# Two FP4 feed-forward stages: quantisation spread over three engines and the gated values quantised two steps later

## The chip, the cores and the metric

The program runs on one core of a Trainium2 chip. The metric is the device time of one execution in microseconds (us). The engines are named as the profile names them: PE is TensorE, PEld its weight loads, DVE VectorE, ACT ScalarE, POOL GpSimd, SP SyncE.

## What is computed

Six stages run one after the other on an activation of 16 x 256 tokens of width 128, each with a layer norm before it and a residual add behind it: an FP4 feed-forward, a low-rank attention, the same FP4 feed-forward again, a mixture of experts, a second attention, the mixture of experts again. The change touches the first and the third stage:

```python
def fp4_quant_dequant(x):                    # blocks of 16 along the last dim
    xb = x.reshape(shape[:-1] + (shape[-1] // BLOCK, BLOCK))
    scale = jnp.maximum(jnp.max(jnp.abs(xb), axis=-1, keepdims=True) / 6.0, 1e-12)
    xn = xb / scale
    idx = jnp.searchsorted(_MID, jnp.abs(xn))
    return (_GRID[idx] * jnp.sign(xn) * scale).reshape(shape)
def fp4_linear(x, w):
    return jnp.einsum('bsk,nk->bsn', fp4_quant_dequant(x), fp4_quant_dequant(w))
gate = fp4_linear(x, w_gate)                 # 128 -> 352
y = fp4_linear(x, w_up)                      # 128 -> 352
h = jax.nn.silu(gate) * y
return fp4_linear(h, w_down)                 # 352 -> 128; x + 0.5 * this
```

## The kernel before

The 4096 tokens are 32 tiles of 128 rows that stay in SBUF (`k.X`). Class `Ffn` handles two tiles at a time, so a run of the stage has N = 16 pairs, and it is called twice (`run` 0 and 1). Every engine has its own program, and semaphores tie them together; the order on each engine is the order in which the code is written. Between two stages all engines meet.

Step z works on the normalised values x of pair z (256 columns) and on the gated values h of pair z - 2 (704 columns) side by side in one buffer of 960 columns, `k.xh`:

- VectorE multiplies silu and the up projection into h (L248), then `quantise` runs over all 960 columns: block maximum (L101), scale (L104), reciprocal (L105), nudge (L106), multiply (L107), absolute value as an integer mask (L114), `max` with the magic number (L115), rounding add (L116). Then it adds the down projection of pair z - 3 to X (L265) and takes its statistics (L184).
- GpSimd subtracts the magic number (L140) and multiplies by the scale (L142), both over 960 columns, into `k.xhq`.
- TensorE transposes x (L293) and h (L299), multiplies by gate and up (L307, into PSUM) and by down (L316).
- ScalarE normalises the next x (L328), copies the transposes to SBUF (L343, L348, L349) and applies silu (L354).

There is one buffer each for the input of quantisation, for the quotient `xn`, for the magnitude `mg` and for the scale. The scale of step z may be written only after GpSimd has ended step z - 1 (`s_scaled`, the wait ahead of L104). A run takes 18 steps.

Of the kernel before, what the change touches and what calls it, by code (L numbers as in the profile page):

```python
# [130 lines left out]
QD = 6  # L131
# [61 lines left out]
class Ffn:  # L193
# [4 lines left out]

    N = NT // 2
    XC, HC_, ALL = (0, 2 * D), (2 * D, 2 * D + 2 * I0), (0, 2 * D + 2 * I0)  # L200

    def __init__(self, k, run):

        self.k, self.run = k, run
        self.x0 = run * self.N
        self.q0 = run * (self.N + 2)
        self.s_xn = k.sem("ffn_xn")
        self.s_xn_read = k.sem("ffn_xn_read")
        self.s_rounded = k.sem("ffn_rounded")
        self.s_minus = k.sem("ffn_minus")  # L210
        self.s_scaled = k.sem("ffn_scaled")
# [10 lines left out]
    def rounds(self, eng, fn, ch=None, per=0):  # L222

        n = self.N
        fn(0, True, False, False)
        fn(1, True, False, False)
        fn(2, True, True, False)
        with eng.Fori(3, n - 1) as z:
            if ch:
                ch.enter(z - 3, per)  # L230
            fn(z, True, True, True)
            if ch:
                ch.leave(n - 4)
        fn(n - 1, True, True, True)
        fn(n, False, True, True)
        fn(n + 1, False, True, True)

    def cols(self, x, h):
        return self.ALL if x and h else self.XC if x else self.HC_

    def vector(self, eng, ch):
        k, v = self.k, self.k.nc.vector
        x0, q0 = self.x0, self.q0

        def fn(z, x, h, back):
            if h:
                eng.wait_ge(self.s_silu, x0 + z - 1)
                v.tensor_tensor(k.xh[:, 2 * D:].rearrange("p (a b) -> p a b", a=2), k.sg[:, :, :],  # L248
                                k.PS[:, 2:4, 0:I0], ALU.mult).then_inc(self.s_h, 1)
                eng.wait_ge(self.s_h, x0 + z - 1)  # L250
# [20 lines left out]
    def gpsimd(self, eng, ch):  # L271
        k = self.k
        x0, q0 = self.x0, self.q0

        def fn(z, x, h, back):
            eng.wait_ge(self.s_rounded, q0 + z + 1)
            if x and (not isinstance(z, int) or z or self.run):
                eng.wait_ge(self.s_xqT_ps, x0 + z)
            if back or (h and self.run):
                eng.wait_ge(self.s_hqT_ps, x0 + z - 2)  # L280
            dequantise(k.nc, k.xhq, k.qt, self.cols(x, h), (self.s_minus, q0 + z + 1), self.s_scaled)

        self.rounds(eng, fn)

    def tensor(self, eng):
        k, t = self.k, self.k.nc.tensor
        x0, q0 = self.x0, self.q0

        def fn(z, x, h, back):
            eng.wait_ge(self.s_scaled, q0 + z + 1)  # L290
            if x:
                for j in range(2):
                    last = t.transpose(k.PS[:, 4, j * P:(j + 1) * P], k.xhq[:, j * D:(j + 1) * D], k.ident[:, :])  # L293
                last.then_inc(self.s_xqT_ps, 1)
            if h:
                for j in range(2):
                    for c, (o, w) in enumerate(HC):
                        o += 2 * D + j * I0
                        last = t.transpose(k.PS[0:w, 5 + j, c * P:(c + 1) * P], k.xhq[:, o:o + w], k.ident[:, :])  # L299
                last.then_inc(self.s_hqT_ps, 1)  # L300
            if x:
                eng.wait_ge(self.s_xqT, x0 + z + 1)
                if not isinstance(z, int) or z or self.run:
                    eng.wait_ge(self.s_h, x0 + z)
                for j in range(2):
                    for w, bank in ((0, 0), (1, 2)):
                        last = t.matmul(k.PS[:, bank + j, 0:I0], k.xqT[:, j * P:(j + 1) * P], k.wguT[:, w, :],  # L307
                                        start=True, stop=True)
# [12 lines left out]

    def scalar(self, eng):
        k, s = self.k, self.k.nc.scalar
        x0, n = self.x0, self.N

        def normalised(i):
            for j in range(2):
                ins = s.activation(k.xh[:, j * D:(j + 1) * D], k.X[:, ds(2 * i + j, 1), :].squeeze(1), ACT.Identity,  # L328
# [4 lines left out]
        normalised(0)  # L333

        def fn(z, x, h, back):
            if x:
                if not (isinstance(z, int) and z == n - 1):
                    eng.wait_ge(self.s_xn_read, x0 + z + 1)
                    normalised(z + 1)
                eng.wait_ge(self.s_xqT_ps, x0 + z + 1)  # L340
                if not isinstance(z, int) or z or self.run:
                    eng.wait_ge(self.s_gu_ps, x0 + z)
                s.activation(k.xqT[:, :], k.PS[:, 4, 0:256], ACT.Copy).then_inc(self.s_xqT, 1)  # L343
            if h:
                eng.wait_ge(self.s_hqT_ps, x0 + z - 1)
                if back:
# [3 lines left out]
            if x:  # L350
                eng.wait_ge(self.s_gu_ps, x0 + z + 1)
                if not isinstance(z, int) or z or self.run:
                    eng.wait_ge(self.s_h, x0 + z)
                s.activation(k.sg[:, :, :], k.PS[:, 0:2, 0:I0], ACT.Silu).then_inc(self.s_silu, 1)  # L354

        self.rounds(eng, fn)
# [800 lines left out]
class Core:  # L1157


    def __init__(self, nc, ctx):  # L1160
        self.nc, self.ctx, self.sems = nc, ctx, {}

        def sb(name, shape, dt=F32):
# [18 lines left out]
        self.sg = sb("sg", [P, 2, I0])  # L1182
        self.hqT = sb("hqT", [P, 2, 3, P])
# [15 lines left out]
                  self.qt["xn"][:, 0:8 * P].rearrange("p (a g c) -> p a g c", a=2, c=32)]  # L1199
        self.mh = self.hqT[:, 0, 0, 0:32].bitcast(BF16).rearrange("p (j r) -> p j r", j=2)  # L1200
# [249 lines left out]
```

## Time and profile before

| | |
|---|---|
| time, median of 3 (lowest, highest) | 2077.7 us (2077.03, 2077.99) |
| the profiled execution's own time | 2078.58 us |
| its span | 2076.8 us |
| feed-forward, first run (first L328 to the end of the last L184) | 172.82 us |
| feed-forward, second run | 174.55 us |
| mean granted TensorE clock, share of full speed | 0.819 |

The span is what the trace covers, and 1.8 us lie around it. A busy time is the sum of an engine's instructions in a stretch; an engine can be idle because it waits for a semaphore, and the timeline shows who released it. The granted clock is 1.0 at full speed and 0.5 at the lower of its two levels.

### The profile page before, as it was taken

Reading aid. Unit: us, or ns where it says so; the run is one execution under the profiler, and the core shown is the slowest. Engines: PE = TensorE matmul, PEld = TensorE weight load, DVE = VectorE, ACT = ScalarE, POOL = GpSimd, SP = SyncE. Lnnn points to the kernel's source line nnn. Section 1 sums busy time; section 2 is a strip of 40 time slices with the busy share of each in tenths; the row PEclk is TensorE's granted clock in tenths of the full one; section 3 lists DMA queues with packets and bytes.
Section 4 is the critical chain, followed back from the end, with each engine's and each line's share of the span. In section 5 each row is a group of like instructions: output and inputs, shape, how many; then the busy total and the mean of one; then the engine's idle time right before and its main releaser. Section 6 shows DMA issues by size and latency. Waiting matters only on the chain. (4 is left out here: it accounts for less than half of the span.)

```text
span 2076.8 us, 34053 instructions
## 1 busy us (share of the span) xinstructions
PE 1307.4 (63%) x10601; PEld 857.0 (41%) x10602; DVE 1045.3 (50%) x2359; ACT 642.3 (31%) x1132; POOL 527.0 (25%) x584
## 2 busy tenths in 40 slices
PE   1565367777755665009999924787878400999991
PEld 1454245455434445005555512454544400555550
DVE  5777556666637773522222255666674352222225
ACT  1222034444442221003333311554555100333330
POOL 1334111111103430562222202121210056222220
PEclk9877578889878885559999966999999555999996
DMA  8400021221200000111111165323231011111114
GB/s 236 64 0 0 18 45 33 40 39 31 47 2 0 0 0 0 33 53 30 35 36 36 36 146 85 63 49 56 41 61 23 0 37 50 32 36 36 36 36 130
DMA packets 194423, 89.80 MB, mean 43 GB/s; under 512 B 128939, under 2 KB 186676, under 8 KB 194356
## 3 DMA queue, kind: packets, MB, share of 16 engines
q1 hardware_dynamic: 185652, 71.02, 16.5%
q0 software_dynamic: 8704, 17.91, 2.4%
q8 instruction: 40, 0.66, 0.1%
q14 instruction: 27, 0.22, 0.0%
HBM read 28.96 MB, written 30.03 MB: 28 GB/s over the span
## 5 line engine op out<-in xcount | busy, mean ns | idle before, releaser
L911 PE MATMUL PS<-wgu,xTs 128*128 x584 | 306.5, 608 | 25.6 <-issue 24.6
L639 ACT ACTIVATE pt<-PS 128x768 f32<-128x768 f32 (+1 forms) x256 | 231.1, 917 | 227.9 <-PE PS L501 227.5
L1018 DVE TENSOR_TENSOR pt<-pt,PS 128x512 f32<-128x512 f32 x146 | 100.4, 688 | 338.5 <-PE PS L911 305.8
L1130 POOL DMA_INDIRECT outs<-ys,xs x144 | 138.0, 958 | 418.0 <-DVE ys L1026 411.8
L718 DVE TENSOR_REDUCE m<-PS 128x4 f32<-128x1024 f32 x128 | 156.3, 1225 | 108.4 <-PE PS L501 107.0
L501 PE MATMUL PS<-tables 64*128 64x192 bf16 (+2 forms) x2048 | 187.3, 264 | 0.0
L718 DVE TENSOR_REDUCE sg<-PS 128x6 f32<-128x768 f32 x128 | 122.0, 956 | 127.7 <-PE PS L501 126.4
L963 ACT ACTIVATE pt<-PS 128x512 f32<-128x512 f32 x146 | 87.2, 597 | 295.0 <-PE PS L911 295.0
L937 PE MATMUL PS<-wdn,pt 128*128 x1152 | 163.5, 285 | 21.4 <-issue 19.1
L1125 POOL DMA_INDIRECT slots<-xr,ix x128 | 123.2, 962 | 211.6 <-DVE ix L1009 190.2
L937 PEld LDWEIGHTS PS<-wdn,pt 128*128 128x128 f32 x1152 | 139.4, 191 | 79.5 <-issue 79.4
L903 PE MATMUL PS<-ident,xs 128*128 128x128 f32 x148 | 41.2, 278 | 193.5 <-DMA xs<-slots 193.3
L140 POOL TENSOR_TENSOR q_mg<-q_xn,q_mg 128x960 f32<-128x960 f32 (+3 forms) x37 | 74.2, 2004 | 284.8 <-DVE q_xn L116 284.8
L958 ACT ACTIVATE xTs<-PS 128x128 f32<-128x128 f32 x148 | 41.1, 278 | 254.0 <-PE PS L903 253.8
L903 PEld LDWEIGHTS PS<-ident,xs 128*128 128x128 f32 x148 | 21.0, 142 | 237.2 <-issue 219.3
L307 PE MATMUL PS<-wguT,xqT 128*128 128x352 f32 x256 | 111.3, 592 | 4.3 <-ACT xqT L343 4.3
L501 PEld LDWEIGHTS PS<-tables 64*128 64x128 bf16 x2048 | 105.8, 103 | 13.6
L519 PE MATMUL PS<-ident,xh 128*128 128x128 f32 x64 | 17.4, 362 | 141.1 <-DVE xh L189 141.1
L911 PEld LDWEIGHTS PS<-wgu,xTs 128*128 128x128 f32 x584 | 90.1, 194 | 36.7 <-issue 36.7
L927 PEld LDWEIGHTS PS<-ident,pt 128*128 128x128 f32 x576 | 72.5, 142 | 76.7 <-issue 75.3
L580 PE MATMUL PS<-pt,v 128*32 128x256 f32 (+1 forms) x1408 | 98.5, 397 | 4.8 <-ACT pt L639 4.5
L293 PE MATMUL PS<-ident,xhq 128*128 128x128 f32 x64 | 17.6, 367 | 130.8 <-POOL xhq L142 130.8
(196 smaller groups left out, 2357.9 us busy)
## 6 DMA issues: line engine op xcount, KB each, us to landing
slots<-empty SPq DMA_DIRECT2D x38, 258.0 KB, 9.9
xs<-slots SPq DMA_DIRECT2D x152, 64.5 KB, 1.8
pt<-outs SPq DMA_DIRECT2D x16, 512.0 KB, 4.2
outs<-ys,xs POOLq DMA_INDIRECT x144, 2.2
wgu<-in_L_ffn_w_gate SPq DMA_DIRECT2D x1, 2048.0 KB
wgu<-in_L_ffn_w_up SPq DMA_DIRECT2D x1, 2048.0 KB
wdn<-in_L_ffn_w_down SPq DMA_DIRECT2D x8, 256.0 KB
qT<-hqT SPq DMA_DIRECT2D x128, 4.0 KB
```

The source lines that it names most:

```text
L140: nc.gpsimd.tensor_tensor(q, t["xn"][:, c], t["mg"][:, c], ALU.subtract).then_inc(minus[0], 1)
L307: last = t.matmul(k.PS[:, bank + j, 0:I0], k.xqT[:, j * P:(j + 1) * P], k.wguT[:, w, :], start=True, stop=True)
L501: last = t.matmul(cols(k.PS[:, self.bank + u, :]), k.eye2[rows, e, :], table[rows], start=False, stop=e == 1, skip_group_check=True)
L580: last = t.matmul(k.PS[32 * u:32 * u + 32, 0, col:col + n], k.v[p][:, kb, g, :], k.pt[:, (2 * a + u // 2) % 4, u % 2, c:c + n], start=kb = ...
L639: s.activation(k.pt[:, a % 4, :, 0:w], k.PS[:, self.bank:self.bank + 2, 0:w], ACT.Exp, scale=self.scale).then_inc(self.s_p, 1)
L718: v.tensor_reduce(out, src, AX.X, ALU.max).then_inc(self.s_nat_read, 1)
L911: t.matmul(k.PS[:, 1 + 2 * p + w, :], k.xTs[:, p, :], k.wgu[:, w, ds(e, 1), :].squeeze(1), start=True, stop=True).then_inc((self.s_gate_ps ...
L937: last = t.matmul(k.PS[:, 6, 0:D], k.hTs[:, p, c * P:(c + 1) * P], k.wdn[:, ds(e, 1), c, :].squeeze(1), start=c == 0, stop=c == FC - 1)
L963: s.activation(k.sgs[:, p, :], k.PS[:, 1 + 2 * p, :], ACT.Silu).then_inc(self.s_silu, 1)
L1018: v.tensor_tensor(k.hs[:, p, :], k.sgs[:, p, :], k.PS[:, 2 + 2 * p, :], ALU.mult).then_inc(self.s_h, 1)
L1125: g.indirect_dma_start(k.slots, bass.IndirectOffsetOnAxis(ap=k.ix[:, u, r:r + 1], axis=0), k.xr[:, u, r, :], None).then_inc(self.s_sc[u], 16)
L1130: g.indirect_dma_start(k.outs, bass.IndirectOffsetOnAxis(ap=k.xs[:, u, D:D + 1].bitcast(I32), axis=0), k.ys[:, u, :], None).then_inc(self. ...
```

## The change

Only `Ffn` and its buffers change.

- Order: step z on VectorE begins with the quantisation of x of pair z and h of pair z - 2 up to the multiply (L262 to L270). Behind it stand the gate of pair z - 1 (L279), the add of pair z - 4 (L293, L184), and last the `max` (L286). A run has 21 steps.
- The absolute value moves to ScalarE (L391, `Abs` with a scale of 2^22), one instruction for both halves, issued one step ahead: `absolute(z + 1)` stands before the silu of step z.
- The rounding add moves to GpSimd, which now makes three passes (add, subtract, multiply) over x (256 columns) and then three over h (704 columns), with a semaphore for each half (`s_xq`, `s_hq`).
- TensorE's step: transposes of x, down projection of pair z - 3, gate and up, transposes of h.
- Two buffers each for the input, `xn`, `mg` and the scale (`fxh`, `fxn`, `fmg`, `fscale`, index z % 2). The second ones lie in memory of the attention's `qT`.
- The loop has two steps in its body.

```diff
+    def walk(self, eng, fn, ch=None, per=0):
+        for z in range(self.FIRST):
+            fn(z, z % 2)
+        passes = (self.N - 2 - self.FIRST) // 2
+        with eng.Fori(0, passes) as m:
...
     def vector(self, eng, ch):
...
+            if x:
+                eng.wait_ge(self.s_xn, x0 + z + 1)
+            if h:
+                eng.wait_ge(self.s_h, x0 + z - 1)
+            ch.run(v.tensor_reduce(amax, blocks, AX.X, ALU.max, apply_absolute_value=True))
+            if x and self.later(z, 2):
+                eng.wait_ge(self.s_xq, x0 + z - 1)
+            if self.has(z - 4) or (h and self.run):
+                eng.wait_ge(self.s_hq, x0 + z - 3)
+            ch.run(v.tensor_scalar(scale, amax, 1.0 / 6.0, 1e-12, ALU.mult, ALU.max))
+            ch.run(v.reciprocal(inv, scale))
+            ch.run(v.tensor_scalar(inv, inv, NUDGE, None, ALU.mult))
+            last = v.tensor_tensor(xn.rearrange("p (n k) -> p n k", k=BLK), blocks,
+                                   inv.unsqueeze(2).broadcast_to([P, n, BLK]), ALU.mult)
+            last.then_inc(self.s_xn_read, 1)
+
+        def fn(z, p):
+            if self.has(z) or self.has(z - 2):
+                quantised(z, p)
+            if self.has(z - 1):
+                eng.wait_ge(self.s_silu, x0 + z)
+                v.tensor_tensor(k.fxh[1 - p][:, HID:k.FW].rearrange("p (a b) -> p a b", a=2), k.sg[:, :, :],
+                                k.PS[:, 2:4, 0:I0], ALU.mult).then_inc(self.s_h, 1)
+            if self.has(z - 4):
+                self.add(eng, z - 4)
+            if self.has(z) or self.has(z - 2):
+                eng.wait_ge(self.s_abs, q0 + z + 1)
+                mg = k.fmg[p][:, 0 if self.has(z) else HID:k.FW if self.has(z - 2) else HID]
+                v.tensor_scalar(mg, mg, MAGIC, None, ALU.max).then_inc(self.s_rounded, 1)
...
     def gpsimd(self, eng, ch):
...
+            ch.run(g.tensor_tensor(xn, xn, mg, ALU.add))
+            ch.run(g.tensor_tensor(mg, xn, mg, ALU.subtract))
+            return g.tensor_tensor(k.xhq[:, c].rearrange("p (n k) -> p n k", k=BLK), mg.rearrange("p (n k) -> p n k", k=BLK),
+                                   k.fscale[:, p, b].unsqueeze(2).broadcast_to([P, b.stop - b.start, BLK]), ALU.mult)
+
+        def fn(z, p):
+            x, h = self.has(z), self.has(z - 2)
+            if x or h:
+                eng.wait_ge(self.s_rounded, q0 + z + 1)
...
+                dequantised(slice(0, HID), p).then_inc(self.s_xq, 1)
...
+                dequantised(slice(HID, k.FW), p).then_inc(self.s_hq, 1)
...
     def scalar(self, eng):
...
+            absolute(z + 1, 1 - p)
+            if self.has(z):
+                eng.wait_ge(self.s_gu_ps, x0 + z + 1)
+                if self.later(z):
+                    eng.wait_ge(self.s_h, x0 + z)
+                s.activation(k.sg[:, :, :], k.PS[:, 0:2, 0:I0], ACT.Silu).then_inc(self.s_silu, 1)
```

TensorE's program, inside the loop. `xhq` holds the dequantised x and h, `wguT` gate and up, `wdT` down. Before:

```order
L293 MATMUL PS<-ident,xhq 128x128 [waits ffn_scaled]
...
L299 MATMUL PS<-ident,xhq 96x128
L307 MATMUL PS<-wguT,xqT 128x352 [waits ffn_h,ffn_xqT]
L307 MATMUL PS<-wguT,xqT 128x352 x3
L311 REGISTER_ALU
L313 REGISTER_ALU [waits ffn_hqT]
L316 MATMUL PS<-wdT,hqT 128x128 [waits ffn_added]
L316 MATMUL PS<-wdT,hqT 128x128 x5
```

And now:

```order
L335 REGISTER_ALU [waits ffn_xq]
L337 MATMUL PS<-ident,xhq 128x128 [waits ffn_xqT]
...
L340 REGISTER_ALU
L342 REGISTER_ALU [waits ffn_hqT]
L345 MATMUL PS<-wdT,hqT 128x128 [waits ffn_added]
L345 MATMUL PS<-wdT,hqT 128x128 x5
L354 MATMUL PS<-wguT,xqT 128x352 [waits ffn_h,ffn_xqT]
L354 MATMUL PS<-wguT,xqT 128x352 x3
L358 REGISTER_ALU
L364 MATMUL PS<-ident,xhq 128x128 [waits ffn_hqT,ffn_hq]
L364 MATMUL PS<-ident,xhq 128x128
...
```

The down projection (L316 before, L345 now) has moved from behind gate and up (L307, L354) to between the transposes of x and gate and up, and the transposes of h (L299, L364) from ahead of gate and up to behind them.

VectorE's program, inside the loop. `fscale` is the scale, `qT` here is a second buffer. Before:

```order
L248 TENSOR_TENSOR xh<-sg,PS 128x704 [waits ffn_silu]
L252 REGISTER_ALU [waits ffn_h]
L101 TENSOR_REDUCE q_amax<-xh 128x60 [waits ffn_xn]
...
L104 TENSOR_SCALAR q_scale<-q_amax 128x60 [waits ffn_scaled,vector_chain]
...
L107 TENSOR_TENSOR q_xn<-xh,q_inv 128x960 [waits vector_chain]
L114 TENSOR_SCALAR q_mg<-q_xn 128x960 [waits ffn_xn_read]
...
L115 TENSOR_SCALAR q_mg<-q_mg 128x960 [waits vector_chain]
...
L116 SCALAR_TENSOR_TENSOR q_xn<-q_xn,q_mg 128x960 [waits vector_chain]
...
L265 SCALAR_TENSOR_TENSOR X<-PS,X 128x256
```

And now:

```order
L262 TENSOR_REDUCE q_amax<-xh 128x60 [waits ffn_h]
...
L266 REGISTER_ALU [waits ffn_xq,vector_chain]
...
L270 TENSOR_TENSOR q_xn<-xh,q_inv 128x960 [waits vector_chain]
...
L279 TENSOR_TENSOR qT<-sg,PS 128x704 [waits ffn_silu]
L293 ISA [waits ffn_y_ps]
L293 SCALAR_TENSOR_TENSOR X<-PS,X 128x256
L184 ISA [waits ffn_added]
L184 BN_STATS bn<-X 128x6
...
L286 TENSOR_SCALAR q_mg<-q_mg 128x960 [waits ffn_abs]
```

The gate (L248, L279) stood at the start of a step and now stands behind the multiply (L107, L270); of the three operations that followed the multiply only the `max` is left (L115, L286), and it stands behind the gate, the add and the statistics.

## Rows read from the trace of the kernel before

**Rows 1.** Busy time by stretch (length, PE, PEld, DVE, ACT, POOL, clock, DMA): both runs.

```profile
38.48:211.30 172.82, 102.60 (x448) 76.28 (x448) 122.23 (x208) 46.07 (x97) 65.30 (x36) 0.81 0.23 33
616.43:790.98 174.55, 103.49 (x448) 76.53 (x448) 122.03 (x208) 46.02 (x97) 65.33 (x36) 0.78 0.00 0
```

**Rows 2.** Timeline, two steps of the first run (start, length, instruction).

```profile
101.20 0.69 PE L293 MATMUL PS<-ident,xhq 128*128 128x128 f32 x2 [6.02 <-POOL xhq L142]
...
102.96 4.53 PE L307 MATMUL PS<-wguT,xqT 128*128 128x352 f32 x8
...
104.85 1.16 DVE L116 SCALAR_TENSOR_TENSOR q_xn<-q_xn,q_mg 128x960 f32<-128x960 f32 x1
...
106.17 2.21 POOL L140 TENSOR_TENSOR q_mg<-q_xn,q_mg 128x960 f32<-128x960 f32 x1 [5.02 <-DVE q_xn L116]
...
108.46 1.82 POOL L142 TENSOR_TENSOR xhq<-q_mg,q_scale 128x960 f32<-128x960 f32 x1
108.99 0.42 DVE L265 SCALAR_TENSOR_TENSOR X<-PS,X 128x256 f32 x1 [2.98 <-PE PS L316]
109.56 0.53 DVE L184 BATCH_NORM_STATS2 bn<-X  x2
110.18 0.89 DVE L248 TENSOR_TENSOR xh<-sg,PS 128x704 f32<-128x704 f32 x1
...
110.34 0.44 PE L293 MATMUL PS<-ident,xhq 128*128 128x128 f32 x2 [1.51 <-POOL xhq L142]
...
111.27 2.62 PE L307 MATMUL PS<-wguT,xqT 128*128 128x352 f32 x8
...
113.72 1.50 PE L316 MATMUL PS<-wdT,hqT 128*128 128x128 f32 x12
...
121.47 0.69 PE L293 MATMUL PS<-ident,xhq 128*128 128x128 f32 x2 [6.25 <-POOL xhq L142]
```

**Rows 3.** Busy time by stretch: pieces of those steps, with the granted clock.

```profile
101.20:107.00 5.80, 5.80 (x15) 4.11 (x16) 4.55 (x7) 1.25 (x3) 0.83 (x1) 0.50 0.00 0
107.00:113.80 6.80, 5.29 (x31) 4.05 (x30) 4.32 (x9) 2.77 (x6) 3.20 (x2) 1.00 0.00 0
115.22:121.40 6.18, 0.00 (x1) 0.00 (x0) 4.75 (x8) 0.46 (x2) 4.02 (x2) 0.66 0.00 0
```

**Rows 4.** Groups by shape, first run: VectorE and ScalarE.

```profile
L107 DVE TENSOR_TENSOR q_xn<-xh,q_inv 128x960 f32<-128x960 f32 x14 | 16.2, 1158 | 0.5
...
L354 ACT ACTIVATE sg<-PS 128x704 f32<-128x704 f32 x16 | 12.1, 758 | 39.4 <-PE PS L307 39.4
...
L115 DVE TENSOR_SCALAR q_mg<-q_mg 128x960 f32<-128x960 f32 x14 | 9.2, 660 | 0.5
...
L639 ACT ACTIVATE pt<-PS 128x1024 f32<-128x1024 f32 x128 | 129.1, 1024 | 103.8 <-PE PS L501 103.6
```

**Rows 5.** Groups by shape, first run: GpSimd.

```profile
L140 POOL TENSOR_TENSOR q_mg<-q_xn,q_mg 128x704 f32<-128x704 f32 x2 | 3.3, 1670 | 8.5 <-DVE q_xn L116 8.5
L142 POOL TENSOR_TENSOR xhq<-q_mg,q_scale 128x704 f32<-128x704 f32 x2 | 2.8, 1385 | 0.2
L140 POOL TENSOR_TENSOR q_mg<-q_xn,q_mg 128x256 f32<-128x256 f32 x2 | 1.4, 724 | 13.1 <-DVE q_xn L116 13.1
L142 POOL TENSOR_TENSOR xhq<-q_mg,q_scale 128x256 f32<-128x256 f32 x2 | 1.2, 621 | 0.2
```

**Rows 6.** Timeline, the end of the first run.

```profile
204.89 1.54 PE L299 MATMUL PS<-ident,xhq 128*128 128x128 f32 x6 [2.69 <-POOL xhq L142]
...
207.38 2.93 PE L316 MATMUL PS<-wdT,hqT 128*128 128x128 f32 x12 [0.95 <-ACT hqT L349]
```

**Rows 7.** Line 700 in the second attention: least, median and most ns of one.

```profile
L700 DVE CAST qs<-xhq x32: 350/353/982, 1256.7 to 1567.3; 128x384 bf16<-128x384 f32 x32
```

**Rows 8.** Timeline, VectorE beside GpSimd in the second attention.

```profile
1256.79 1.80 POOL L765 TENSOR_TENSOR ks<-xhq,gone 128x384 bf16<-128x384 f32 x2 [14.01 <-ACT xhq L627]
...
1257.94 0.80 DVE L704 TENSOR_TENSOR dq<-xhq,qs 128x128 f32<-128x128 f32 x1
```

More of the change, by code:

```diff
@@ L220, in __init__, with has, later @@
         self.s_added = k.sem("ffn_added")
[L222 to L228, printed above, removed]
+    def has(self, i):
+        return not isinstance(i, int) or 0 <= i < self.N
+    def later(self, i, n=1):
+        return self.run or not isinstance(i, int) or i >= n
+    def walk(self, eng, fn, ch=None, per=0):
[3 more added lines that the diff above has]
+        with eng.Fori(0, passes) as m:
@@ L229, in rounds @@
             if ch:
-                ch.enter(z - 3, per)
-            fn(z, True, True, True)
+                ch.enter(m, 2 * per)
+            for i in range(2):
+                fn(2 * m + (self.FIRST + i), i)
             if ch:
[L233 to L239, printed above, removed]
+                ch.leave(passes)
@@ L241, in vector @@
+        for z in range(self.FIRST + 2 * passes, self.STEPS):
+            fn(z, z % 2)
     def vector(self, eng, ch):
         k, v = self.k, self.k.nc.vector
[L243 to L250, printed above, removed]
+        x0, q0, HID = self.x0, self.q0, self.HID
@@ L251, in fn, with quantised @@
+        def quantised(z, p):
+            x, h = self.has(z), self.has(z - 2)
+            c = slice(0 if x else HID, k.FW if h else HID)
+            b = slice(c.start // BLK, c.stop // BLK)
+            n = b.stop - b.start
+            src, xn, mg, scale = k.fxh[p][:, c], k.fxn[p][:, c], k.fmg[p][:, c], k.fscale[:, p, b]
+            blocks = src.rearrange("p (n k) -> p n k", k=BLK)
+            amax, inv = k.qt["amax"][:, b], k.qt["inv"][:, b]
             if x:
                 eng.wait_ge(self.s_xn, x0 + z + 1)
-            free = (self.s_scaled, q0 + z) if not isinstance(z, int) or z or self.run else None
@@ L262, in add @@
+        self.walk(eng, fn, ch, 4)
     def add(self, eng, i):
@@ L271, in gpsimd, with dequantised, fn @@
     def gpsimd(self, eng, ch):
[L272 to L283, printed above, removed]
+        k, g = self.k, self.k.nc.gpsimd
+        x0, q0, HID = self.x0, self.q0, self.HID
+        def dequantised(c, p):
+            b = slice(c.start // BLK, c.stop // BLK)
+            xn, mg = k.fxn[p][:, c], k.fmg[p][:, c]
+            ch.run(g.tensor_tensor(xn, xn, mg, ALU.add))
[3 more added lines that the diff above has]
+        def fn(z, p):
+            x, h = self.has(z), self.has(z - 2)
+            if x or h:
+                eng.wait_ge(self.s_rounded, q0 + z + 1)
+            if x:
+                if self.later(z):
+                    eng.wait_ge(self.s_xqT_ps, x0 + z)
+                dequantised(slice(0, HID), p).then_inc(self.s_xq, 1)
+            if h:
+                if self.later(z - 2):
+                    eng.wait_ge(self.s_hqT_ps, x0 + z - 2)
+                dequantised(slice(HID, k.FW), p).then_inc(self.s_hq, 1)
+        self.walk(eng, fn, ch, 4)
     def tensor(self, eng):
         k, t = self.k, self.k.nc.tensor
-        x0, q0 = self.x0, self.q0
-        def fn(z, x, h, back):
-            eng.wait_ge(self.s_scaled, q0 + z + 1)
+        x0, HID = self.x0, self.HID
+        def fn(z, p):
+            x, h, down = self.has(z), self.has(z - 2), self.has(z - 3)
             if x:
+                eng.wait_ge(self.s_xq, x0 + z + 1)
+                if self.later(z):
+                    eng.wait_ge(self.s_xqT, x0 + z)
                 for j in range(2):
@@ L349, in fn @@
                 s.activation(k.hqT[0:96, :, 2, :], k.PS[0:96, 5:7, 256:384], ACT.Copy).then_inc(self.s_hqT, 1)
[L350 to L356, printed above, removed]
+        self.walk(eng, fn)
 class Attention:
```

81 lines of the change are left out of this document (48 added, 33 removed).

## The prediction

> **What bounds the kernel now.** I read the two feed-forward runs alone, since no other stage's instructions change. They take 172.82 and 174.55 us [rows 1], 347.4 together. No engine fills them: VectorE is busy for 122 of 173 us, TensorE 103, GpSimd 65, ScalarE 46. Next I read the timeline of two steps [rows 2]. One TensorE step starts at 101.20, the next at 110.34, the one after at 121.47: 9.1 and 11.1, 10.13 us on average. The reader is to see how the steps hang together: the rounding add ends at 106.01, GpSimd subtracts from 106.17 to 108.38, multiplies from 108.46 to 110.28, and TensorE starts its transposes at 110.34. While GpSimd works, VectorE does the add, statistics and gate, then prepares the next step. It is the engine that most of the step is spent on, and one buffer between it and GpSimd makes them take turns for part of it.
>
> The same matmuls cost very different times. Gate and up take 4.53 us in one step and 2.62 in the next [rows 2]. The granted clock says why: it is 0.50 (1.2 GHz) from 101.20, when TensorE comes back to work, to 107.00, then 1.00 (2.4 GHz) to 113.80; over the next idle stretch, 115.22 to 121.40, its mean is 0.66, so it falls during that one [rows 3]. An idle stretch of 6 us costs full speed, the 1.5 us ahead of 110.34 did not.
>
> **What the change takes away.** On VectorE the absolute value and the rounding add, 0.66 (taken from the `max`, of equal shape) and 1.16 us a step [rows 2, 4], together 1.8, and the wait for GpSimd ahead of the scale. Its work per step, 122 us over 16 pairs or 7.6 [rows 1], falls to 5.8. GpSimd gets one more pass: x now costs 0.72 + 0.72 + 0.62, h 1.67 + 1.67 + 1.39 [rows 5], 6.8 us, with five gaps of 0.08 (108.38 to 108.46) 7.2 us. ScalarE gets an `Abs` over 960 columns: between silu over 704 in 0.76 and 1024 columns in 1.02 [rows 4], I take 0.97. By busy time alone every engine would be under 8 us a step. What decides is the order.
>
> **The ring that the new order closes.** In step z GpSimd starts x of pair z when VectorE's `max` of step z is done. TensorE transposes it, then does the down projection of pair z - 3, then gate and up; ScalarE applies silu; VectorE multiplies the gate, adds pair z - 4, takes the statistics, and only then comes `max` of step z + 1. None of these can be overtaken, since each engine follows its written order, and second buffers don't cut any link. At the full clock:
>
> - `max` 0.66 [rows 4], then 0.16 to GpSimd (106.01 to 106.17) [rows 2]: 0.82
> - x on GpSimd 0.72 + 0.08 + 0.72 + 0.08 + 0.62 [rows 5], 0.06 to TensorE: 2.28
> - TensorE: transposes 0.44, down 1.50, gate and up 2.62 [rows 2]: 4.56. ScalarE's copy of x lies under the down projection: between transposes and gate and up it left 0.49 (110.78 to 111.27).
> - silu 0.76 [rows 4] with 0.03 ahead: 0.79
> - gate 0.89, add 0.42, statistics 0.53 [rows 2], with gaps of 0.03, 0.03, 0.15 and 0.09: 2.14
>
> The sum is 10.6 us, already over the 10.13 of now, which include steps at the low clock. Down (1.50) lay behind gate and up before, outside this path; add and statistics lay under GpSimd's work.
>
> **TensorE's clock.** Between the end of gate and up and the next transposes lie 0.79 + 2.14 + 0.82 + 2.28 = 6.0 us, in which TensorE has only the transposes of h, 0.8 us at their start. So about 5.2 us idle in every step, where now every other step has a long one. I expect the clock to fall in nearly all of them. All of the work at the low clock: transposes 0.69, gate and up 4.53 [rows 2], down 2.93 [rows 6], 8.15, that is 3.6 more. If the low clock lasts 5.80 us into the work as at 101.20 [rows 3], 5.80 / 8.15 = 71% is done at it, the rest in 1.3 us: 2.6 more. The idle stretch is a little shorter than the one in the rows and now and then the clock will still be high when work begins, so I take 1.9, with 0 and 3.6 as bounds.
>
> **VectorE and GpSimd side by side.** Before, in this stage, they overlapped only in operations that read PSUM or one tensor. Now scale, nudge, multiply run beside GpSimd's passes. The second attention shows what such a pair does: a cast that takes 350 ns at least takes up to 982 [rows 7]; one VectorE `tensor_tensor` that starts at 1257.94, while GpSimd works until 1258.59, takes 0.80 us and ends 0.15 after GpSimd [rows 8]. It waits for the other to finish. Here that makes VectorE's chain from `max`: GpSimd starts after 0.16; scale waits for its subtract (1.68), nudge for the first pass over h (4.2), multiply for the second (5.9) and ends at 7.0; `Abs` 1.0; silu 0.8; gate, add and statistics 2.0; `max` 0.7: 11.5 at most, close to the ring at the full clock and under the ring at 12.5. On the ring itself it costs only what GpSimd waits for scale, 0.2 (bounds 0 and 0.5).
> The Trainium skill, "SBUF — State Buffer", section "Who interferes with whom", has this as a rule: VectorE in a two-port mode or with two SBUF inputs and GpSimd exclude one another for a whole instruction. By that rule the step at the full clock would be 11.3 to 11.5, without it 10.6; the rows just named agree, and at the low clock it changes nothing.
>
> **The sum.** A full step: 10.6 + 1.9 + 0.2 = 12.7 us. A run:
>
> - to the end of `max` of step 0: 3.3 us, an estimate (seven short operations and two normalisations, each 0.2 to 0.9)
> - three steps with neither down nor add: 10.6 + 0.2 - 1.50 - 0.42 - 0.53 - gaps 0.2 = 8.2, plus 2.0 for transposes and gate and up at the low clock: 10.2 each, 30.6
> - twelve full steps: 152.4
> - the `max` of the first step without x (its predecessor still has it): 12.0; that of the last: GpSimd's add and subtract 3.6, then multiply, `Abs`, `max` 2.5, add and statistics 1.1 and gaps: 7.6
> - the drain: GpSimd over h 4.9 + 0.2, transposes to the end of down 204.89 to 210.31, 5.4 [rows 6], add and statistics 1.0: 11.5
>
> 217.4 us, against 172.82 and 174.55. Two runs: 434.8 - 347.4 = +87.4. On the profiled execution's 2078.6 us this gives 2166.0; the median lies 0.9 under that execution, so 2165. The other stages are free of it: `qT` is used again only after all engines met.
>
> **The rivals.**
> - The forecast, clock low in part of each step: chance 0.72. Of its own, 1.2 to 2.6 for the clock and 0.5 for the blocking give 2145 to 2190.
> - The clock stays high, since TensorE now works in each step and no idle stretch reaches 6 us. For it: the stretch is 5.2, not 6.2. Against it: it is far nearer to 6 than to 1.5. Step 10.6 to 11.3, a run 181 to 194: +15 to +40, 2092 to 2118. Chance 0.14.
> - The clock is low throughout: for it that TensorE is busy for only 4 to 5 of 10 us; against it 107.00 to 113.80. Step 14.4, a run 239: +130, 2208. Chance 0.06.
> - Other side: `max` doesn't wait for the gate in effect, because silu and gate of step z are done before VectorE arrives. Then the busiest engine sets the step: GpSimd's 7.2 and blocking by VectorE's two-input multiply (1.16) [rows 4] and three smaller ones, about 0.9, makes 8.8 to 9.3. Twelve such steps, three of 8, and 33 for head and tail: 163 to 169 a run, -9 to -21, 2057 to 2069. It decides as soon as the ring is under 9.3 us; the ring would have to lose 1.3 us even at the full clock. Chance 0.07.
> - Nothing changes: 0.01.
>
> A measurement of this kernel tells 0.2% (4 us) from no change. From the cases: faster 0.07, same 0.01, slower 0.92. The range must leave out no more than 0.2: from 2110, which takes in the upper half of the high-clock case, to 2192.
>
> **What would show it.** In the changed trace GpSimd's first pass over x should start 0.16 behind each `max`, the starts should lie 11.8 to 13.2 us apart, silu should wait for gate and up and not for `Abs`, and VectorE should wait for silu in each step. The granted clock over the stage should fall from 0.8 to about 0.75 or less, and be 0.50 where the transposes of x start. The multiply should take about 2.6 us beside GpSimd instead of 1.16. I am wrong if the starts lie under 10.5 us apart, above all if the clock stays at 1.00; then the clock was the mis-sized term.

## The result, and the profile after

The changed kernel takes 2151.4 us (median of 4 runs, 2148.5 to 2153.9) against 2077.4 (4 runs, 2076.1 to 2078.0). The ratio is 1.0354, with a 95% interval of 1.0339 to 1.0368: 74 us slower. The profiled execution took 2151.2 us, its span 2149.4.

The page's first part (busy time, share of the span, instructions by engine) after the change:

```profile
PE 1337.5 (62%) x10601; PEld 880.5 (41%) x10602; DVE 1028.9 (48%) x2287; ACT 672.5 (31%) x1168; POOL 637.0 (30%) x704
```

Nothing in it looks like a bound: no engine is busier than 62%. The loss is in the order, and stands in the stretches. Busy time by stretch (length, PE, PEld, DVE, ACT, POOL, clock, DMA) of both feed-forward runs, then of three pieces of two steps:

```profile
38.57:247.56 208.99, 118.96 (x448) 88.37 (x448) 114.26 (x172) 61.09 (x115) 120.77 (x96) 0.77 0.19 28
653.15:861.99 208.84, 118.21 (x448) 88.02 (x448) 114.20 (x172) 61.30 (x115) 120.75 (x96) 0.74 0.00 0
...
112.35:117.94 5.59, 5.59 (x22) 4.40 (x22) 2.51 (x2) 2.15 (x4) 5.40 (x3) 0.72 0.00 0
117.94:123.59 5.65, 0.89 (x7) 0.63 (x7) 4.47 (x9) 1.62 (x3) 2.11 (x4) 0.88 0.00 0
123.59:130.38 6.79, 6.79 (x24) 5.32 (x25) 2.61 (x2) 2.15 (x4) 5.48 (x3) 0.59 0.00 0
```

The runs now take 208.99 and 208.84 us, 417.8 together, where they took 347.4 [rows 1]: +70.5 of the 72.6 us by which the spans differ. VectorE does less (114 us for 122), GpSimd nearly twice as much (121 for 65), ScalarE 61 for 46. The timeline of the changed kernel shows two steps, and the `max` at either end of twelve (start, length, instruction, in brackets the idle time before and what ended it):

```profile
73.21 0.65 DVE L286 TENSOR_SCALAR qT<-qT 128x960 f32<-128x960 f32 x1
...
109.19 0.64 DVE L286 TENSOR_SCALAR q_mg<-q_mg 128x960 f32<-128x960 f32 x1
...
109.99 0.72 POOL L306 TENSOR_TENSOR q_xn<-q_xn,q_mg 128x256 f32<-128x256 f32 x1 [4.56 <-DVE q_mg L286]
110.79 0.72 POOL L307 TENSOR_TENSOR q_mg<-q_xn,q_mg 128x256 f32<-128x256 f32 x1
...
111.59 0.62 POOL L308 TENSOR_TENSOR xhq<-q_mg,fscale 128x256 f32<-128x256 f32 x1
...
112.16 0.19 DVE L269 TENSOR_SCALAR q_inv<-q_inv 128x60 f32<-128x60 f32 x1
...
112.35 0.69 PE L337 MATMUL PS<-ident,xhq 128*128 128x128 f32 x2 [5.15 <-POOL xhq L308]
112.39 2.51 DVE L270 TENSOR_TENSOR qT<-qT,q_inv 128x960 f32<-128x960 f32 x1
...
112.82 2.76 PE L345 MATMUL PS<-wdT,hqT 128*128 128x128 f32 x12
...
113.96 2.48 POOL L307 TENSOR_TENSOR q_mg<-q_xn,q_mg 128x704 f32<-128x704 f32 x1
115.02 1.00 ACT L391 ACTIVATE qT<-qT 128x960 f32<-128x960 f32 x1 [0.73 <-DVE qT L270]
...
115.38 2.56 PE L354 MATMUL PS<-wguT,xqT 128*128 128x352 f32 x8
...
117.99 0.76 ACT L408 ACTIVATE sg<-PS 128x704 f32<-128x704 f32 x1 [1.96 <-PE PS L354]
118.78 0.89 DVE L279 TENSOR_TENSOR xh<-sg,PS 128x704 f32<-128x704 f32 x1 [3.88 <-ACT sg L408]
...
119.58 0.42 DVE L293 SCALAR_TENSOR_TENSOR X<-PS,X 128x256 f32 x1
120.15 0.53 DVE L184 BATCH_NORM_STATS2 bn<-X  x2
120.60 0.64 DVE L286 TENSOR_SCALAR qT<-qT 128x960 f32<-128x960 f32 x1
...
123.59 0.69 PE L337 MATMUL PS<-ident,xhq 128*128 128x128 f32 x2 [4.76 <-POOL xhq L308]
...
126.63 3.75 PE L354 MATMUL PS<-wguT,xqT 128*128 128x352 f32 x8
...
131.21 0.89 DVE L279 TENSOR_TENSOR qT<-sg,PS 128x704 f32<-128x704 f32 x1 [4.98 <-ACT sg L408]
...
133.03 0.64 DVE L286 TENSOR_SCALAR q_mg<-q_mg 128x960 f32<-128x960 f32 x1
...
215.80 0.64 DVE L286 TENSOR_SCALAR qT<-qT 128x960 f32<-128x960 f32 x1
```

Read the first step from `max` to `max` (L286, from 109.19 to 120.60). It starts at 109.19; GpSimd adds, subtracts and scales x (L306 to L308) from 109.99 to 112.21; TensorE transposes x, does the down projection (L345) and gate and up (L354) from 112.35 to 117.94; silu (L408) starts 0.05 later, the gate (L279) right behind it, then add (L293) and statistics (L184), and at 120.60 the next `max`. Each instruction of this chain starts when the one before it on the list ends, on whichever engine that was. That is a ring: 11.41 us. The next, to 133.03, takes 12.43; the only link that differs by more than 0.1 us is gate and up, 3.75 for 2.56. The granted clock is 0.50 over 112.35 to 115.38 and 0.99 over the gate and up behind it; in the next step it is 0.50 from 123.59 to 128.50, into gate and up. Twelve steps, from the `max` at 73.21 to that at 215.80, take 11.88 us on average, where the kernel before had 10.13 [rows 2].

The waits of the first run (engine, what waited, for what; us in total, times, longest):

```profile
ACT sg L408 <- PE PS L354: 44.2, 16, 5.2
DVE qT L279 <- ACT sg L408: 42.5, 8, 7.1
...
DVE xh L279 <- ACT sg L408: 35.0, 8, 7.6
```

VectorE waits 77.5 us for silu in its 16 gates; silu waits 44.2 us for gate and up. `Abs` (L391) ends at 116.02, 4.58 us before `max` needs it.

### The profile page after: what moved, and what is told of

Read it like the earlier page. It is cut to its first block, busy times and chain, and to the rows that moved or that the text cites. A ratio compares the mean times of both kernels' runs of the same rounds, so it can differ in the third digit from the quotient of the medians.

```text
span 2149.4 us, 34091 instructions
## 1 busy us (share of the span) xinstructions
PE 1337.5 (62%) x10601; PEld 880.5 (41%) x10602; DVE 1028.9 (48%) x2287; ACT 672.5 (31%) x1168; POOL 637.0 (30%) x704
## 4 chain that ended last, share of the span: by engine, by line
PE 44%; DVE 11%; issue 9%; POOL 8%; DMA 5%; SPq 4%; ACT 2%; DVEq 1%; POOLq 0%; ACTq 0%
PE PS L971 12%; PE PS L997 7%; POOL slots L1185 4%; PE PS L640 4%; PE PS L987 3%; PE PS L354 2%; PE PS L561 2%; SPq L869 2%; DMA qT<-qs 2%; PE PS L609 2%; PE PS L345 2%; DVE m L778 2%; PE PS L625 2%; DMA slots<-xr,ix 1%; PE PS L936 1%
## 5 line engine op out<-in xcount | busy, mean ns | idle before, releaser
L337 PE MATMUL PS<-ident,xhq 128*128 128x128 f32 x64 | 21.9, 446 | 166.3 <-POOL xhq L308 166.3
L354 PE MATMUL PS<-wguT,xqT 128*128 128x352 f32 x256 | 112.2, 597 | 2.8 <-ACT xqT L399 2.8
L825 POOL TENSOR_TENSOR ks<-r,gone 128x192 bf16<-128x192 f32 x32 | 15.8, 514 | 300.5 <-DVE r L750 300.5
```

## The experiments

My theory is the ring. Its rivals are the things that the change also did: three passes on GpSimd instead of two, VectorE and GpSimd that now stop one another, `Abs` on ScalarE, and TensorE's clock. Times are medians of 4 executions (10 for busy_tensor); edits are of the changed kernel unless said otherwise. Each ratio is to the kernel before as timed beside that kernel: 2077.9 us for down_behind, max_first, add_on_vector and add_vector_max_first, 2081.2 for busy_tensor, before_busy_tensor, tuned_cover and tuned_fold, 2077.8 for the other four. Medians of kernels from different groups can so be compared to some 4 us only; the text gives their plain differences. The rest of the program, which no edit touches, differs from one profiled execution to another by more than some of the effects (from the second run's last matmul to the end of the span it is 1281 to 1293 us). So beside each median stands a finer measure: from the first matmul of gate and up to the last of the down projection in TensorE's timeline, the two feed-forward runs added up ("the runs").

| kernel | median us | ratio to before | the runs, us |
|---|---|---|---|
| before | 2077.4 | | 332.6 |
| changed | 2151.4 | 1.0354 | 401.3 |
| down_behind | 2129.3 | 1.0260 | 384.7 |
| max_mid | 2118.2 | 1.0181 | 375.6 |
| max_first | 2059.2 | 0.9908 | 315.1 |
| busy_tensor | 2089.5 | 1.0045 | 342.5 |
| before_busy_tensor | 2061.3 | 0.9921 | 311.6 |
| add_on_vector | 2159.3 | 1.0405 | 411.1 |
| add_vector_max_first | 2052.7 | 0.9878 | 306.2 |
| mask_on_vector | 2152.3 | 1.0334 | 403.2 |
| tuned_cover | 2055.3 | 0.9891 | 302.5 |
| tuned_fold | 2040.9 | 0.9828 | 296.4 |
| tuned_mask | 2058.9 | 0.9898 | 312.6 |
| tuned_mask_busy | 2056.8 | 0.9899 | 311.6 |

### Links of the ring, cut one at a time

**down_behind.** On TensorE the down projection goes back behind gate and up, out of the ring.

```diff
-            if down:
-                eng.wait_ge(self.s_hqT, x0 + z - 2)
...
             if x:
                 eng.wait_ge(self.s_xqT, x0 + z + 1)
...
+            if down:
+                eng.wait_ge(self.s_hqT, x0 + z - 2)
...
             if h:
```

> The changed kernel (2151 us, 11.41 and 12.43 us a step by turns), with the down projection of pair z - 3 behind gate and up again instead of ahead of them. Ring theory: 1.5 to 2.8 us of matmuls leave the path from max to max; VectorE's multiply and the absolute value then come close behind, so 0.8 to 1.4 us a step are won, 2110 to 2128 us. Rival, that VectorE and GpSimd blocking each other is the cost: nothing on TensorE matters, 2145 to 2157 us.

2129.3 us, interval 1.0232 to 1.0289: 22 us better, 17 of them in the runs. That is 0.6 us for each of the 26 steps that have both (13 a run), less than the 0.8 to 1.4 expected (the time is 1 us over the range), although up to 2.77 us of matmuls left the ring. TensorE's timeline says why; here L345 is gate and up, L354 down:

```profile
111.55 4.04 PE L345 MATMUL PS<-wguT,xqT 128*128 128x352 f32 x8 [0.55 <-ACT xqT L399]
...
115.43 1.50 PE L354 MATMUL PS<-wdT,hqT 128*128 128x128 f32 x12
...
122.40 5.06 PE L345 MATMUL PS<-wguT,xqT 128*128 128x352 f32 x8 [0.47 <-ACT xqT L399]
...
127.25 1.90 PE L354 MATMUL PS<-wdT,hqT 128*128 128x128 f32 x12
```

Gate and up takes 4.04 and 5.06 us where it took 2.56 and 3.75. In the changed kernel the down projection stood in the slow part of TensorE's work; now gate and up stands there. And TensorE now idles 0.55 and 0.47 us ahead of gate and up, until ScalarE has copied x (L399); in the changed kernel that copy lay under the down projection. So of the 2.8 us some 1.4 went back in slower matmuls and 0.5 in this wait.

**max_mid.** `max` goes between gate and add, so that only add and statistics leave the ring.

```diff
+            if self.has(z) or self.has(z - 2):
+                eng.wait_ge(self.s_abs, q0 + z + 1)
+                mg = k.fmg[p][:, 0 if self.has(z) else HID:k.FW if self.has(z - 2) else HID]
+                v.tensor_scalar(mg, mg, MAGIC, None, ALU.max).then_inc(self.s_rounded, 1)
             if self.has(z - 4):
                 self.add(eng, z - 4)
-            if self.has(z) or self.has(z - 2):
...
```

> The changed kernel with VectorE's max between the gate and the add of pair z - 4 instead of behind the statistics. Ring theory: add and statistics, 1.0 us with their gap, leave the ring and nothing else does: 0.9 to 1.1 us a step, 2114 to 2125 us. If the order on VectorE behind the gate doesn't matter: 2148 to 2155 us.

2118.2 us, interval 1.0151 to 1.0211, as the ring theory had it: 33 us better, 26 of them in the runs, 1.0 for each of the 26 steps with an add. In the changed kernel 0.93 lay between the end of the gate (119.67) and `max` (120.60).

**max_first.** `max` goes right behind the multiply, ahead of silu's wait. This opens the ring.

```diff
                 quantised(z, p)
+            if self.has(z) or self.has(z - 2):
+                eng.wait_ge(self.s_abs, q0 + z + 1)
...
             if self.has(z - 1):
                 eng.wait_ge(self.s_silu, x0 + z)
...
-            if self.has(z) or self.has(z - 2):
-                eng.wait_ge(self.s_abs, q0 + z + 1)
...
```

> The changed kernel with VectorE's max of step z right behind its multiply, ahead of the gate, the add and the statistics; nothing else moves. Ring theory: max no longer waits for silu, the ring is open, and what is left is VectorE with its waits for GpSimd, about 10 us a step: 2070 to 2095 us. Rival, blocking alone: the same operations still block each other, over 2135 us.

2059.2 us, interval 0.9888 to 0.9927: 92 us better than the changed kernel, 18 better than the kernel before (86 and 17 in the runs), and 11 under the range I had given. Not one instruction is gone; four lines stand a few lines higher. This alone gives back more than the whole loss of 74. The granted clock comes back too: 0.89 over 100 to 170, where the changed kernel has 0.79. With the ring open the next limit shows in the timeline:

```profile
110.21 0.69 DVE L280 TENSOR_SCALAR q_mg<-q_mg 128x960 f32<-128x960 f32 x1 [1.07 <-ACT q_mg L391]
...
114.99 1.67 POOL L307 TENSOR_TENSOR q_mg<-q_xn,q_mg 128x704 f32<-128x704 f32 x1
...
115.56 1.15 DVE L269 TENSOR_SCALAR q_inv<-q_inv 128x60 f32<-128x60 f32 x1
...
116.74 2.41 POOL L308 TENSOR_TENSOR xhq<-q_mg,fscale 128x704 f32<-128x704 f32 x1
116.75 1.16 DVE L270 TENSOR_TENSOR qT<-qT,q_inv 128x960 f32<-128x960 f32 x1
...
119.06 0.66 DVE L280 TENSOR_SCALAR qT<-qT 128x960 f32<-128x960 f32 x1 [1.16 <-ACT qT L391]
```

VectorE's nudge (L269) over 60 columns, 0.19 us in the changed kernel, takes 1.15: it ends 0.05 us after GpSimd's subtract (L307, 114.99 to 116.66). Then GpSimd's scale of h (L308), 1.39 us when alone, takes 2.41 beside the multiply. And `max` (L280) stands 1.1 us behind `Abs`.

### The clock

**busy_tensor.** Six matmuls whose result nobody reads, 2.76 us of TensorE at full speed, in the idle stretch behind the transposes of h.

```diff
                 last.then_inc(self.s_hqT_ps, 1)
+            if x:
+                for _ in range(6):
+                    t.matmul(k.PS[:, 4, 256:512], k.ident[:, :], k.wguT[:, 0, 0:256], start=True, stop=True)
```

> The changed kernel with six more matmuls of 256 columns behind TensorE's transposes of h in each step, whose result nothing reads; they fill the idle stretch ahead of the next transposes of x. It computes nothing else. Clock theory: the clock stays at 1.0 where x arrives, and transposes, down, gate and up take 4.6 us instead of 5.6 and 6.8, so the step falls from 11.9 to 10.3 to 10.9: 2095 to 2122 us. If the clock has no part in it, 2148 to 2160 us.

2089.5 us, interval 1.003 to 1.0061: 62 us better (59 in the runs), with more work, and 5 us under the range I had given. Busy time by stretch, of 100 us and of TensorE's part of one ring:

```profile
100.00:200.00 100.00, 78.06 (x410) 59.28 (x409) 71.10 (x103) 36.27 (x68) 77.36 (x61) 1.00 0.00 0
102.89:107.06 4.17, 4.17 (x22) 2.97 (x22) 2.53 (x2) 2.15 (x4) 4.03 (x2) 1.00 0.00 0
```

The clock is 1.00 (2.4 GHz) over these 100 us (0.96 and 0.94 over the whole of the two runs), and transposes, down, gate and up take 4.17 us instead of 5.59 and 6.79. The steps take 9.80 and 9.98. So the ring at the full clock is 9.9, and the low clock costs 2.0 a step, 1.4 and 2.6 by turns: 59 us over 30 steps.

**before_busy_tensor.** The same six matmuls in the kernel before, behind its down projection.

```diff
                 last.then_inc(self.s_y_ps, 1)
+                for _ in range(6):
+                    t.matmul(k.PS[:, 4, 256:512], k.ident[:, :], k.wguT[:, 0, 0:256], start=True, stop=True)
```

> The kernel before with six such matmuls behind the down projection. Clock theory: the steps that start at the low clock lose part of their 2 us, and the long idle stretch is shorter, so 3 to 7 us a run of the stage are won: 2062 to 2073 us. If VectorE and GpSimd taking turns sets the step, or if the clock falls all the same: 2074 to 2082 us.

2061.3 us, interval 0.989 to 0.9951: 1 us under the range; the kernel before loses some 16 us to the clock as well, 21 by the runs. Busy time over 80 us, and the start of VectorE's reduction (L101) in three steps:

```profile
100.00:180.00 80.00, 65.98 (x355) 52.27 (x356) 66.06 (x107) 24.18 (x52) 34.23 (x18) 1.00 0.00 0
```

```profile
144.48 1.15 DVE L101 TENSOR_REDUCE q_amax<-xh 128x60 f32<-128x960 f32 x1
...
153.63 1.15 DVE L101 TENSOR_REDUCE q_amax<-xh 128x60 f32<-128x960 f32 x1
...
162.77 1.15 DVE L101 TENSOR_REDUCE q_amax<-xh 128x60 f32<-128x960 f32 x1
```

The steps are an even 9.15 us, where they were 9.1 and 11.1 [rows 2]. There the clock cost 0.7 us a step on average (21 over 32; 1.0 in the steps shown), in the ring 2.0, where every matmul is waited for.

### GpSimd's third pass

**add_on_vector.** The rounding add goes back to VectorE, in the order of the changed kernel.

```diff
-                v.tensor_scalar(mg, mg, MAGIC, None, ALU.max).then_inc(self.s_rounded, 1)
...
+                ch.run(v.tensor_scalar(mg, mg, MAGIC, None, ALU.max))
+                v.tensor_tensor(xn, xn, mg, ALU.add).then_inc(self.s_rounded, 1)
...
-            ch.run(g.tensor_tensor(xn, xn, mg, ALU.add))
```

> The changed kernel with the rounding add on VectorE behind the max again, GpSimd with two passes; order and buffers as changed. Ring theory: the add (1.16 us) goes onto the ring and GpSimd's first pass over x (0.72 + 0.08) leaves it, so about 0.4 us a step more: 2155 to 2172 us. Rival, blocking: the multiply no longer waits for a pass of 1.7 us, and one pass of 1.67 is gone, so 1 us a step or more is won: under 2125 us.

2159.3 us, interval 1.0385 to 1.0424: 8 us worse, 10 in the runs. In the ring only x counts, and there GpSimd's add over 256 columns is shorter than VectorE's over all 960. The blocking of the two engines moves but is there all the same, in VectorE and GpSimd side by side:

```profile
111.12 1.68 POOL L308 TENSOR_TENSOR q_mg<-q_xn,q_mg 128x704 f32<-128x704 f32 x1
...
111.81 1.04 DVE L269 TENSOR_SCALAR q_inv<-q_inv 128x60 f32<-128x60 f32 x1
...
112.87 1.39 POOL L309 TENSOR_TENSOR xhq<-q_mg,fscale 128x704 f32<-128x704 f32 x1
112.88 2.39 DVE L270 TENSOR_TENSOR qT<-qT,q_inv 128x960 f32<-128x960 f32 x1
```

The nudge (L269) now ends 0.05 after GpSimd's subtract (L308, to 112.80), the multiply (L270, 1.16 alone) takes 2.39 beside GpSimd's scale (L309). All of it lies under TensorE's work.

**add_vector_max_first.** This, with `max` and the add behind the multiply as in max_first.

> Both edits: max and rounding add on VectorE right behind the multiply and ahead of the gate. Ring theory, with blocking as the second limit: with the ring open the step is VectorE's own work of 7.0 us and the waits for GpSimd that are left, about 8.9 us: 2040 to 2065 us, under both kernels and 20 to 45 below max_first. If blocking costs nothing once the ring is open, the extra 1.16 us on VectorE makes it slower than max_first.

2052.7 us, interval 0.9855 to 0.9901: inside the range, but only 6 us better than max_first, 9 in the runs, where I had expected 20 or more. With the ring open the third pass on GpSimd costs, but little.

### The absolute value

**mask_on_vector.** `Abs` on ScalarE goes; VectorE clears the sign bit behind the multiply, in the order of the changed kernel.

```diff
+            eng.wait_ge(self.s_xn_read, q0 + z + 1)
+            ch.run(v.tensor_scalar(mg.bitcast(I32), xn.bitcast(I32), 0x7FFFFFFF, None, ALU.bitwise_and))
...
-                v.tensor_scalar(mg, mg, MAGIC, None, ALU.max).then_inc(self.s_rounded, 1)
+                v.tensor_scalar(mg, mg, 2.0 ** 22, MAGIC, ALU.mult, ALU.max).then_inc(self.s_rounded, 1)
...
-            absolute(z + 1, 1 - p)
...
```

> The changed kernel with the absolute value on VectorE again, as an integer mask right behind the multiply; ScalarE's instruction is gone. Ring theory: VectorE waits 3.9 us for silu there, the 0.66 us lie in that wait, and silu waits for gate and up, not for the absolute value: 2145 to 2157 us. If ScalarE's extra 1.00 us ahead of silu, or the engine it is on, counts: under 2135 us. If VectorE's work counts: over 2165 us.

2152.3 us, interval 1.0295 to 1.0373: 1 us from the changed kernel, 2 in the runs. VectorE's mask (L274) and gate (L281):

```profile
114.61 2.02 DVE L274 TENSOR_SCALAR qT<-qT 128x960 int32<-128x960 int32 x1
118.50 0.89 DVE L281 TENSOR_TENSOR xh<-sg,PS 128x704 f32<-128x704 f32 x1 [1.88 <-ACT sg L398]
```

The mask takes 2.02 us beside GpSimd, and VectorE still waits 1.88 for silu. In the ring this work has room on either engine.

### Versions with the ring open

**tuned_cover.** add_vector_max_first, with the add of pair z - 4 and the statistics between multiply and `max`, to cover VectorE's wait for `Abs`.

> The version with max and rounding add on VectorE ahead of the gate (2052.7 us), with the add of pair z - 4 and its statistics moved between the multiply and the max, where VectorE now waits 1.07 us for ScalarE's absolute value. If that wait counts: up to 1 us a step, 2020 to 2035 us. If VectorE only comes to GpSimd's passes earlier and waits there instead: 2045 to 2057 us.

2055.3 us, interval 0.9861 to 0.9921. By the runs 4 us are gained on add_vector_max_first, by the median none: the gain is too small to stand out from the rest of the program. The wait for `Abs`, 1.1 us, is gone, and VectorE waits inside its small instructions instead. GpSimd's scale of h (L309), the nudge (L269) and the multiply:

```profile
114.33 1.39 POOL L309 TENSOR_TENSOR xhq<-q_mg,fscale 128x704 f32<-128x704 f32 x1
...
114.90 0.87 DVE L269 TENSOR_SCALAR q_inv<-q_inv 128x60 f32<-128x60 f32 x1
115.80 1.16 DVE L270 TENSOR_TENSOR qT<-qT,q_inv 128x960 f32<-128x960 f32 x1
```

**tuned_fold.** The same with the nudge folded into the multiply, one instruction fewer between GpSimd's passes. The two factors are multiplied in another order, so the last bit of a product can differ.

```diff
-            ch.run(v.tensor_scalar(inv, inv, NUDGE, None, ALU.mult))
-            last = v.tensor_tensor(xn.rearrange("p (n k) -> p n k", k=BLK), blocks,
-                                   inv.unsqueeze(2).broadcast_to([P, n, BLK]), ALU.mult)
+            last = v.scalar_tensor_tensor(xn.rearrange("p (n k) -> p n k", k=BLK), blocks, NUDGE,
+                                          inv.unsqueeze(2).broadcast_to([P, n, BLK]), ALU.mult, ALU.mult)
```

> As the one before, and the nudge is folded into the multiply as its scalar, so VectorE issues no separate instruction for it. That takes away 0.23 us of work and one of the places where VectorE waits for a pass of GpSimd (0.86 and 1.15 us were seen on an instruction of 0.19 us). Blocking theory: 0.5 to 0.9 us a step less than the one before, 15 to 28 us. If only its own length counts: 7 us less.

2040.9 us, interval 0.9795 to 0.986: the fastest of all, 36 us under the kernel before (36 by the runs too) and 110 under the changed one. By the median it is 14 us under tuned_cover, but only 6 of these are in the runs (the rest of the program took 1281 us in one trace and 1292 in the other): steps of 8.6 instead of 8.85, which is the nudge's own 0.19 and little more. That is the rival of the expectation, 7 us less, and not the 15 to 28 of the blocking theory. I had expected the meeting with GpSimd to go with it. It moved into the next instruction:

```profile
111.01 1.68 POOL L307 TENSOR_TENSOR q_mg<-q_xn,q_mg 128x704 f32<-128x704 f32 x1
...
111.65 1.08 DVE L267 TENSOR_SCALAR fscale<-q_amax 128x60 f32<-128x60 f32 x1
...
112.76 1.38 POOL L308 TENSOR_TENSOR xhq<-q_mg,fscale 128x704 f32<-128x704 f32 x1
...
113.33 1.83 DVE L269 SCALAR_TENSOR_TENSOR qT<-qT,q_inv 128x960 f32<-128x960 f32 x1
```

The scale (L267) over 60 columns still takes 1.08 us and ends 0.04 behind GpSimd's subtract (L307, 112.69). The multiply takes 1.83 and ends 1.02 behind GpSimd's scale (L308, 114.14), where in tuned_cover it took 1.16 and ended 1.24 behind it. The changed kernel's multiply, 2.51 long, also ended 1.02 behind the pass that it met (L306, 113.88). So some 0.7 of the 1.83 is waiting, if the folded instruction takes the same 1.16 when alone; no row shows it alone.

**tuned_mask.** tuned_fold with the mask on VectorE in place of ScalarE's `Abs`.

> The version with the folded nudge (2040.9 us), with the mask on VectorE behind the multiply in place of ScalarE's absolute value. With the ring open VectorE sets the step, so now its own work counts: 0.66 us more, and the wait for ScalarE of up to 1.07 us, which the add and statistics only cover in part, is gone: 2032 to 2052 us; the theory names no sign here.

2058.9 us, interval 0.987 to 0.9927: 18 us above tuned_fold by the medians, 15 by the ratios (16 by the runs, 0.5 a step), and 7 beyond the range I gave. With the ring open a step is made of VectorE's work, and most of the mask's 0.66 us is paid. Moving the absolute value to ScalarE is worth 15 to 18 us there, and nothing in the ring.

**tuned_mask_busy.** tuned_mask with four unread matmuls a step, as in busy_tensor.

> As the one before, with four unread matmuls of 256 columns behind the transposes of h in each step. With the ring open TensorE is off the path, so the clock should hardly matter here, unlike in the changed kernel, where six of them took 62 us: within 12 us of the one before.

2056.8 us, interval 0.9867 to 0.9931: 2 us from tuned_mask, 1 by the runs. This alone tests little, since the four matmuls hardly raised the granted clock: 0.90 and 0.86 over the two runs, where tuned_mask has 0.87 and 0.80. But tuned_mask's own trace shows that the clock doesn't count there. From 66 to 160 us its gate and up takes from 2.53 to 3.91 us, and yet VectorE's reductions (L262) start 9.33 to 9.42 us apart in all ten steps. Whether it counts in max_first, where the steps vary from 8.0 to 10.6 us, was not tried.

## Why the prediction was right

It said 2165 us with a range of 2110 to 2192, and slower; 2151.4 is in the range, 14 us below. The mechanism was the ring with the clock low in part of each step, and max_first shows it: opening the ring takes 92 us away. It also builds the condition of the rival on the other side, for which the prediction worked out 2057 to 2069: 2059.2. In the step shown there GpSimd sits idle for only 0.65 of 8.75 us, as that rival had it (8.8 to 9.3 a step); but the run's steps vary from 8.0 to 10.6, 9.4 on average, so that the time fits so well is in part luck. busy_tensor builds that of the rival with the clock kept high, 2092 to 2118: 2089.5, just under it. Term by term, forecast and then measured, the mean of the two steps shown:

- `max` to GpSimd 0.82, measured 0.76; x on GpSimd to the transposes 2.28, measured 2.31 with the blocking in it.
- Blocking on the ring 0.2, measured about 0: L308 starts 0.08 behind L307 at 111.59, as unblocked passes do. Off the ring the multiply takes 2.51 us for 1.16, as forecast, and GpSimd's subtract over h 2.48 for 1.67 [rows 4, 5], hidden under TensorE. But it meets an earlier pass: the nudge, which was to wait out GpSimd's add over h, starts 0.01 ahead of it (112.16) and isn't held, and the multiply ends 5.1 us behind `max` and not 7.0. So VectorE's own chain lay further under the ring than the prediction had it. They go by turns: the multiply (to 114.90) ends 1.02 behind GpSimd's add (to 113.88), the subtract (to 116.44) 1.54 behind the multiply. "It waits for the other to finish" holds for both.
- TensorE 4.56 and 1.9 for the clock, 6.46; measured 6.19. At the full clock it is 4.17, not 4.56. I had summed three times of separate rows that overlap at their edges. The clock is 2.0, near the forecast 1.9 in part by luck: I took less than the 2.6 worked out, since in some steps the clock might still be high when work begins. It never was (the transposes of x take the 0.66 to 0.69 us of the low clock in every full step, where busy_tensor's take 0.43), but in every second step it rose after 3.0 us of work, so that 1.4 and 2.6 took turns.
- silu 0.79, measured 0.83.
- Gate, add, statistics 2.14, measured 1.82. I had added four gaps, but instructions of VectorE start up to 0.09 us before the one ahead has ended (119.58, 120.60).

Together 11.9 for 12.7. **The step of the prediction that was off is a size: the mis-sized term is the ring at the full clock: 9.9 us measured, 10.8 with the blocking forecast.** Twelve steps took 142.6 us for 152.4, a run 209 for 217: two runs are 17 us under the 434.8 forecast. The other parts of a run nearly offset one another: 35.3 for 33.9 to the end of step 3's `max`, 12.3 for 12.0 to the first `max` without x, 6.1 for 7.6 to the last, 12.7 for 11.5 of drain. Outside the runs the span grew by 2.1 us, which I had put at nothing and can't place.

Of what was to be seen in the trace, GpSimd's first pass over x starts 0.16 and 0.08 behind the end of `max` in the two steps shown, where 0.16 was forecast; silu's wait for gate and up, VectorE's for silu and the low clock at the transposes of x (0.69 us, as in [rows 2]) came as said. The starts were to lie 11.8 to 13.2 apart: their mean does, but every second one is 11.4. The stage's clock was to be 0.75 or less: it is 0.77 and 0.74.

The cuts don't add up: down 22, add and statistics 33, clock 62, but all of it 92. No cut can win more than the way down to the next limit, which in max_first is VectorE and GpSimd with their waits for one another and for `Abs`. The split of down_behind between clock, copy and matmuls was read from its trace and not tried with the clock kept high.

## What to carry to other kernels

Before you put second buffers between engines, follow one item round all of them and back to its first engine: if the written order makes step z + 1 wait on each engine for step z, buffers cut nothing, and the period is the sum of the links and not the busiest engine. Then move the instruction that closes the ring (here four lines, 92 us) before you move work between engines; what such a move is worth depends on it (the rounding add on GpSimd gained 8 us in the ring and lost 6 outside; the absolute value on ScalarE gained nothing in the ring and some 16 outside). And measure an effect of some us in its own stage: the rest of the program moved by as much between kernels that share it.

## What the runs showed of the hardware

- VectorE's scale and nudge (`tensor_scalar`) on only 60 columns wait until GpSimd's pass has ended, and the wait shows inside their duration, not as idle time: 0.19 us became 1.15, ending 0.05 us after GpSimd. The reciprocal between them, on the same 60 columns, doesn't wait: it keeps its 0.53 us beside GpSimd's subtract (L268 in max_first). GpSimd waits in the same way: 1.67 became 2.48, and 1.39 became 2.41. The add from PSUM (L293 in max_first) kept its 0.42 us, and the reduction its 1.15, beside GpSimd's passes. The Trainium skill, "SBUF — State Buffer", section "Who interferes with whom", has VectorE in a two-port mode or with two SBUF inputs and GpSimd exclude one another for a whole instruction, and the one issued first keep the other out. The rows of the multiply, which has two inputs, and of the reduction agree; the scale and the nudge have one input, and in which mode they ran no row shows.
- Six unread matmuls a step in the idle stretch held the clock at 1.00 in the middle of a run and made both kernels faster, the changed one by 62 us, the one before by 16. Four of them in tuned_mask left it at 0.90 and 0.86 over the runs and did nothing that can be told (2 us).
- The part of the program behind the second run, the same in all fourteen kernels, took from 1281 to 1293 us in their profiled executions. Its cause wasn't looked for.
